# Attention with a low-rank FFN on one core: where the row maxima are turned, and which of three PSUM banks each product gets

## What is computed

```
def attention(q, k, v):                      # q: layernorm(x), k = v = context
    qh = q.reshape(B, S, KV, G, D)           # KV 8, G 4, D 32, S 512
    scores = einsum('bkgsd,bktd->bkgst', qh, kh) / sqrt(D)
    return einsum('bkgst,bktd->bkgsd', softmax(scores), vh)
x = x + attention(layernorm(x), ctx, ctx)
x = x + ffn(layernorm(x))   # gates of 8 experts, the best one's rank-8 update, bias, debias
```

## Time and profile before

| | us |
|---|---|
| median of 3 runs (lowest to highest) | 1023.52 (1023.04 to 1024.38) |
| the profiled execution's own time | 1017.48 |
| its span, first to last instruction | 1015.7 |
| busy: PE 940.9, DVE 901.5, POOL 801.3, ACT 726.1 | of 1015.7 |

### The profile page before, as it was taken

One profiled execution on the slowest core, in us unless ns is written; L12 is line 12 of the kernel. 1 busy time (PEld: TensorE's weight loads), 2 busy tenths in 40 slices (PEclk: granted clock), 3 DMA queues, 4 the chain that ended last, 5 costly groups with the idle time before them and its releaser, 6 DMA issues.

```text
span 1015.7 us, 24586 instructions
## 1 busy us (share of the span) xinstructions
PE 940.9 (93%) x9518; PEld 368.9 (36%) x9518; DVE 901.5 (89%) x1106; ACT 726.1 (71%) x1301; POOL 801.3 (79%) x454
## 2 busy tenths in 40 slices
PE   4799999999999999999999999999999999999996
PEld 3223333333333333333333323333222225777773
DVE  6979999999999999999999999998888886888877
ACT  5378888888888888887777777788777777554440
POOL 7269999999999999999999999998999998322210
PEclk9789999999999999999999999999999999999999
DMA  7685686768676768676767686756556744766424
GB/s 248 198 179 122 149 184 143 178 137 184 139 176 148 182 133 187 134 177 147 185 142 174 141 185 132 182 121 153 120 123 138 163 92 152 236 222 221 169 109 165
DMA packets 319875, 164.18 MB, mean 162 GB/s; under 512 B 182216, under 2 KB 307240, under 8 KB 319760
## 3 DMA queue, kind: packets, MB, share of 16 engines
q1 hardware_dynamic: 319456, 161.76, 64.8%
q0 software_dynamic: 304, 0.85, 0.4%
HBM read 107.58 MB, written 54.53 MB: 160 GB/s over the span
## 4 chain that ended last, share of the span: by engine, by line
PE 36%; DVE 30%; issue 24%; ACT 5%; POOL 3%; DMA 0%; SPq 0%; DVEq 0%; POOLq 0%; ACTq 0%
DVE row_max L927 14%; PE psum L590 8%; PE psum L604 6%; PE psum L617 5%; PE psum L735 4%; DVE den_t L939 4%; PE psum L552 4%; ACT probs L864 4%; PE psum L713 3%; DVE o_t L933 2%; DVE probs L1138 2%; PE psum L578 2%; DVE prod_mem L985 2%; PE psum L701 1%; ACT prod_mem L817 1%
## 5 line engine op out<-in xcount | busy, mean ns | idle before, releaser
L864 ACT ACTIVATE probs<-psum 128x512 f32<-128x512 f32 x1024 | 552.8, 596 | 134.9 <-PE psum L590 121.7
L927 DVE TENSOR_REDUCE row_max<-psum 128x4 f32<-128x2048 f32 x248 | 565.1, 2279 | 65.9 <-PE psum L552 65.5
L590 PE MATMUL psum<-q_stack,k_stack 97*32 97x512 f16 x4096 | 329.7, 386 | 7.7 <-ACT probs L864 2.1
L353 POOL TENSOR_TENSOR sums<-probs 128x2048 f32<-128x2048 f32 x63 | 287.3, 4561 | 17.4 <-ACT probs L864 17.4
L365 POOL TENSOR_TENSOR sums<-probs 128x2048 f32<-128x2048 f32 x63 | 287.9, 4570 | 13.0 <-ACT probs L864 12.9
L604 PE MATMUL psum<-probs,v_in 128*32 128x512 f32 x2048 | 268.2, 598 | 3.9 <-ACT probs L864 0.2
L590 PEld LDWEIGHTS psum<-q_stack,k_stack 97*32 97x32 f16 x4096 | 91.4, 94 | 219.6 <-ACT probs L864 131.4
L552 PE MATMUL psum<-high_mem 32*128 32x512 f16 x992 | 98.2, 385 | 23.6 <-DVE row_max L927 20.0
L325 POOL TENSOR_TENSOR o_t<-o_t,inv 128x512 f32<-128x512 f32 x64 | 67.2, 1050 | 32.1 <-DVE inv L945 32.1
L604 PEld LDWEIGHTS psum<-probs,v_in 128*32 128x32 f32 x2048 | 58.1, 110 | 87.2 <-issue 54.3
L330 POOL TENSOR_TENSOR o_all<-o_all,o_t 128x512 f32<-128x512 f32 x64 | 81.5, 1273 | 9.2
(11 more groups left out here) (119 smaller groups left out, 762.4 us busy)
## 6 DMA issues: line engine op xcount, KB each, us to landing
q_stack<-q_split SPq DMA_DIRECT2D x192, 128.0 KB, 3.5
xa<-in_x_dram SPq DMA_DIRECT2D x32, 512.0 KB, 4.9
o_all<-in_x_dram SPq DMA_DIRECT2D x256, 64.0 KB, 2.4
x_attended<-o_all SPq DMA_DIRECT2D x64, 256.0 KB, 4.2
out_dram<-probs SPq DMA_DIRECT2D x32, 512.0 KB, 2.8
q_split<-prod_mem SPq DMA_DIRECT2D x15, 1024.0 KB, 5.3
xa<-x_attended SPq DMA_DIRECT2D x16, 512.0 KB, 4.4
probs<-x_attended SPq DMA_DIRECT2D x16, 512.0 KB, 4.7
```

The source lines that it names most:

```text
L353: pool.tensor_tensor(sums[:, (2 * u - 1) % SUMS], probs[:, (u - 1) % 2, 2], probs[:, (u - 1) % 2, 3], ALU.add).then_inc(back_done, 1)
L590: last = pe.matmul(st_ps[row:row + D, bank_of["score", u, n], :], k_stack[:, u % SLOTS, t * P + row:t * P + row + D], q_stack[:, u % SLOTS ...
L864: act.activation(probs[:, s, keys, g, :], st_ps[:, bank_of["score", u, n], :], ACT.Exp, scale=EXP_SCALE).then_inc(exped, 1)
L927: dve.reduce_max(row_max[:, u % 2, t:G * ST:ST], s_ps[:], AX.X).then_inc(reduced, 1)
```

## The change

`turn_max(u+1)` moves, in TensorE's third quarter, from behind the gather to right behind the maxima product; `make_shift` moves in ScalarE's stream from the middle of the third quarter's exponentials to the beginning of that quarter, ahead of the part's high half. The planner is rewritten: instead of counting uses (a score keeps its bank for 2 further uses, a part for 6), it gives each use a time in quarters and a number of quarters that it is kept (0.4 for a score or the maxima, 0.95 for a part; denominators until a given point of the next unit), and a tile's second and third part need no longer be in the bank of the part before. Nothing is computed otherwise.

```
-            filled = [("part", n, i) for n in range(FIRST) for i in range(PIECES)]
+            QUARTERS_KEPT = {"score": 0.4, "max": 0.4, "part": 0.95}
+            DEN_TAKEN_AT = (ST + 0.95, 3.95)
+            filled = [(-LEAD, ("part", n, i)) for n in range(FIRST) for i in range(PIECES)]
...
-                    if u % 2 == 1 and t < PIECES and whole(tile_of(u)):
-                        filled.append(("part", tile_of(u), t))
-                    filled += scores[:half]
-                    if t == 2 and live(u + 1):
-                        filled.append(("max", u + 1, 0))
-                    filled += scores[half:]
+                    now = []
+                    if t == 2 and live(u + 1):
+                        now.append(("max", u + 1, 0))
+                    if u % 2 == 1 and t < PIECES and whole(tile_of(u)):
+                        now.append(("part", tile_of(u), t))
+                    now += scores
...
+                    filled += [(u * ST + t + (i + 1) / (len(now) + 1), use) for i, use in enumerate(now)]
...
-                if use[0] == "part" and use[1] >= FIRST and use[2] > 0:
-                    bank = bank_of["part", use[1], use[2] - 1]
...
-                kept = KEPT["den"][use[1] % 2] if use[0] == "den" else KEPT[use[0]]
-                free_at[bank], last_in[bank] = max(i, free_at[bank]) + kept + 1, use
+                if use[0] == "den":
+                    free_at[bank] = (use[1] + 1) * ST + DEN_TAKEN_AT[use[1] % 2]
+                else:
+                    free_at[bank] = max(at, free_at[bank]) + QUARTERS_KEPT[use[0]]
+                last_in[bank] = use
...
@@ tensor
+                        if t == 2 and 0 < u + 1 < UNITS:
+                            turn_max(u + 1)
                         if u % 2 == 1 and t < PIECES and whole(tile_of(u)):
                             turn_part(tile_of(u), t)
...
                             gather(u, t - 1)
-                        if t == 2 and 0 < u + 1 < UNITS:
-                            turn_max(u + 1)
@@ scalar
+                        if t == 2 and live(u + 1):
+                            make_shift(u + 1)
                         if u % 2 == 1 and t < PIECES and whole(tile):
                             high_part(tile, t)
...
-                                if n == MIDST[u % 2][2] and live(u + 1):
-                                    make_shift(u + 1)
```

More of the change, by code:

```diff
@@ L204, in xattn_ffn @@
                     scores = [("score", u, n) for n in range(BEGIN[u % 2][t], BEGIN[u % 2][t + 1])] if live(u) else []
-                    half = MIDST[u % 2][t] - BEGIN[u % 2][t]
+                    now = []
+                    if t == 2 and live(u + 1):
+                        now.append(("max", u + 1, 0))
                     if u % 2 == 1 and t < PIECES and whole(tile_of(u)):
-                        filled.append(("part", tile_of(u), t))
-                    filled += scores[:half]
-                    if t == 2 and live(u + 1):
-                        filled.append(("max", u + 1, 0))
-                    filled += scores[half:]
+                        now.append(("part", tile_of(u), t))
+                    now += scores
                     if t == (ST - 1 if u % 2 == 1 else 2) and live(u - 1):
-                        filled.append(("den", u - 1, 0))
-            KEPT = {"score": 2, "max": 2, "den": (5, 5), "part": 6}
-            bank_of, bank_before, free_at, last_in = {}, {}, [0] * BANKS, [None] * BANKS
-            for i, use in enumerate(filled):
+                        now.append(("den", u - 1, 0))
+                    filled += [(u * ST + t + (i + 1) / (len(now) + 1), use) for i, use in enumerate(now)]
+            bank_of, bank_before, free_at, last_in = {}, {}, [-LEAD] * BANKS, [None] * BANKS
+            for i, (at, use) in enumerate(filled):
                 bank = min(range(BANKS), key=lambda b: free_at[b])
-                if use[0] == "part" and use[1] >= FIRST and use[2] > 0:
-                    bank = bank_of["part", use[1], use[2] - 1]
                 bank_of[use] = bank
@@ L865, in _ @@
                                                scale=EXP_SCALE).then_inc(exped, 1)
-                        elif t == 2 and live(u + 1):
-                            make_shift(u + 1)
                 def copy_yT(q, t):
```

## The result

The changed kernel takes 1008.84 us (median of 4 runs, 1008.09 to 1009.29), the kernel before beside it 1023.28 us (4 runs, 1017.98 to 1024.38): 0.9866 of it, with a 95% interval of 0.9848 to 0.9884. The profiled execution took 1008.09 us. Against the profiled execution of before (1017.48) that is 9.4 us, which looks like the forecast.

What follows compares the result with a forecast made beforehand. VectorE (23.59 us) and TensorE (24.23) were both near their limit in a 25.30 us pair. Pairs 7.5, late pairs 0.1 and unit 0 1.0 sum to 8.6, taken as 8.7: 1023.52 to 1014.8 us, range about 1011 to 1020.5.

Steps and rivals of the forecast that it cites:

- odd unit, 25 times: Odd unit's third and fourth quarter: maxima product and gather come sooner, gaining 0.28 us (0.17 to 0.38) per unit.
- even unit, 25 times: Even unit's third quarter: 0.21 + 0.06 - 0.29 = -0.02 us, bounds -0.23 to +0.05.
- late pairs: The six pairs without a part, behind the 25: only the even unit's term counts, 0.1 us.
- three banks in unit 0: Unit 0: a third bank removes scores' standing for exponentials, 0.5 us at each of two places, 1.0 us (0 to 1.2).
- none is waited for in the pair, so I cost them at nothing: SyncE's queue: shift's DMA up to 1.4 us (even) and 2.0 us (odd) sooner, what queues behind it too; counted as nothing.
- I charge 0.20 us: Odd unit: cost of the turned maxima running ahead of the part, bounds 0.10 and 0.31 us.
- neighbouring consideration: Odd unit: changing tiling mode drains TensorE, so turned maxima would cost 0.12 us, not 0.20; total about 2 us better.
- for a reason that the profile cannot show: Base: timed median 1023.52 us lies 6.04 us above the profiled execution, unexplained; the gain was taken from the median.
- its lower end, about 1011: Fast end of the range: 1023.5 - 25 x 0.45 - 1.2, about 1011 us.
- The slower rival: Odd unit's score 9 waits for a late shift, holding TensorE, from 0.78 us of lateness; about 1027 us, chance 0.06.
- the brake on ScalarE: Odd unit: exponentials 8 and 9 slip by 0.31 us or more, only 3 to 4 us gained, 1019.5 us; chance 0.18.
- A stretch at half clock: From the nothing-moves rival (0.10): a second such stretch in the run costs up to 8.5 us, eating the gain; 1023 us.

Runs made afterwards that it cites:

- even_only: The kernel before with the turned maxima moved in even units alone, banks by the old rules: 1018.57 us, 0.9961.
- plan_only: The kernel before with only the new planner, turned maxima and shift's copy in their old places: 1023.24 us, 1.0009.
- shift0_sooner: The kernel before with only ScalarE's copy of unit 0's shift put ahead of the part's high half: 1018.76 us, 0.9968.
- move_old_start: The kernel before with both moves and the old planner, but unit 0's shift copy left behind the part's high half: 1007.94 us, 0.9856.
- move_only: The kernel before with only the moves of the turned maxima and the shift's copy, old planner's bank rules: 1005.36 us, 0.9827.
- three_banks: The kernel before with both moves, old planner, unit 3's load behind unit 1's shift, and unit 0's scores in three banks: 1002.92 us, 0.9807.
- unit3_later: The changed kernel with unit 3's first load taken out of SyncE's start and put behind unit 1's shift: 1007.6 us, 0.9854.
- before_profiled: The kernel before, unchanged, run once more for a second profile: 1021.41 us, 0.9989, profiled at 1022.17 us.
- max_bank: The changed kernel with an odd unit's turned maxima taking the second bank to come free instead of the first: 1006.69 us, 0.9841.

## Why the prediction was wrong

The mechanism was right: the odd unit's waits are the ones named, the shift hides, ScalarE is no brake, and nothing in the pair waits for the shift. The sum was too small. By its terms:

| term | forecast, us | shown, us | by |
|---|---|---|---|
| odd unit, 25 times | 25 x 0.28 = 7.0 | 25 x 0.31 = 7.8 | timeline after |
| even unit, 25 times | 25 x 0.02 = 0.5 | 25 x 0.10 = 2.5 | even_only, timeline after |
| late pairs | 0.1 | 0.5 | six times 24.09 to 24.00 |
| three banks in unit 0 | 1.0 | 0 | plan_only |
| SyncE, unit 0's shift | 0 | 3.3 (1.6 to 4.8) | shift0_sooner, move_old_start |
| sum | 8.6, taken as 8.7 | 14.1 | measured 14.4 by the medians, 13.7 (11.9 to 15.6) by the ratio |

The pairs' terms are firm to a tenth; the 3.3 us are not, so the sum's closeness to the measured time is partly luck.

- **The step that failed most** is "none is waited for in the pair, so I cost them at nothing". It is true in the pairs and was carried to the start, where SyncE's queue has no pause and each issue behind unit 0's shift, unit 1's shift among them, inherits its time. A DMA is hidden only as long as its queue has slack, and I looked for slack where the kernel spends its time, not where it begins. By the medians the effect is larger than the 0.3 to 0.9 us by which unit 1's shift goes out sooner (58.13, against 58.45 and 59.05 in the two profiles of before); how long TensorE stands and whether a stretch at half clock follows go with it. How the 3.3 us divide between the start and the tail is not settled: against the second profile of before, that of shift0_sooner is 2.2 us shorter up to unit 2 and 1.2 in the tail, against the recorded one 0.5 shorter and 1.7 longer. Without this term the others give 10.8 us, about 1012.5, inside the range.
- **The even unit** gave 0.10 us and not 0.02. Every row that I read was right (0.33, 0.21, 0.06 measured as 0.07); the term left out is the 0.08 us of the first denominators, which stood for the bank of the turned maxima. I followed what is queued behind the moved instruction, and not who takes its bank next. The explanation by the bank rests on the rows and the bank tables; the experiment shows only that the gain belongs to the even half.
- **The odd unit**: "I charge 0.20 us" for the turned maxima ahead of the part was too much, they cost 0.12. Exactly that stood in the neighbouring consideration by the Trainium skill, page "TensorEngine Tiling (Array Packing)", section Key Properties; the trace agrees with the number, 440.05 to 440.17, and no run isolates the reason. The maxima product came 0.18 us sooner for 0.11 forecast, the following one 0.31 for 0.28, and VectorE's idle time fell to 0.39 and 0.22 for 0.46 and 0.18.
- What the prediction took as given, that the turned maxima must wait for the low half, is the changed planner's choice and costs the 0.12 us. With the old rules (move_only) the odd half gives 0.44.
- **Unit 0**: "so both count: 1.0 us" failed. VectorE did wait for TensorE there, but behind it stood a third party, the shift of unit 1 in SyncE's queue, which took the gain (the stand of 4.86 us in plan_only). Where that was out of the way, three_banks shows 0.5 us that is the banks' and up to 1.25 together with a sooner rise of the clock; whether 1.0 was the right size is open.
- **The base**: that the profiled execution lies 6 us under the median "for a reason that the profile cannot show" was given up too early. Its windows show 4.7 us of it beside a second profile: no stand of 2.8 us at the start and no half clock in the tail. The forecast of the span, about 1007 with 1006.3 measured, was right by luck: the gain was forecast too small, and the execution that it was taken from was faster than most.
- **The range**: its lower end, about 1011, was worked out with 0.45 us a pair, though the bound given for a pair was 0.61; with 0.61 and the same 1.2 it is about 1007, and the measured time lies inside. The slower rival's 1027 does not follow from its terms either: at 1 us of lateness, with 0.40 of slack and the 0.30 gained, they give about 1031. Nothing rests on that one.
- **The rivals**: for the brake on ScalarE to hold, exponentials would have had to slip; six run in a row from 441.33. For the slower case the shift would have had to come 0.78 us late; its copy starts 0.30 us behind the turned maxima's start (440.05) and is done at 440.62, ahead of the high half. A stretch at half clock does exist at 60.8, but the kernel before has one as well in its second profile.

## What to carry to other kernels

Cost a change to a queue at nothing only where the queue is seen to pause, and look at the start apart from the steady state: there one DMA that goes out sooner moves everything behind it, and a load taken out of the way of one transfer may land in front of the next, as in unit3_later. When an operation moves, follow its buffer as well as its engine: who had to wait for it, and which use it must now wait for; a planner that picks banks by time of release alone can put a cheap instruction behind a late reader although a free bank stands beside it. And take a second profile of the baseline, or at least split it into stretches, before a difference of two profiles is read as a gain.

## What the runs showed of the hardware

- The tail, the same instructions in all these kernels, comes in three lengths: 186.12 us in the recorded profile of before with no stretch at half clock, 187.53 in that of the changed kernel with one of 3.4 us, 189.10 in before_profiled with one of 6.8 us. The other eleven profiles fall beside one of the three (185.9, 187.2 to 187.8, 188.7 to 189.1). What decides which one comes is open; it would account for 3 of the 6 us over which the runs of one kernel spread.
- Seven stands of TensorE for unit 1's shift, 2.28 to 4.86 us long, were each followed by 3.4 or 6.8 us at half clock, three of 0.69 to 1.25 us by none; but the stand of 2.39 us for unit 2's shift in unit3_later was followed by none.
- A shift's transfer of 4 KB landed 2.3 to 2.8 us behind its issue for unit 1, but for unit 2 anywhere from 1.7 us (before_profiled, plan_only, max_bank) to 4.6 (move_only), with 3.7 in the changed kernel and in unit3_later. Why it varies is open.
- In the windows before the first record of the clock PEclk reads 1.00, though the durations tell of half clock. The first maxima products of the changed kernel take longer than the later ones of the same shape, the first of these lines against the second:

```profile
47.56 0.61 PE L544 MATMUL psum<-high_mem 32*128 32x512 f16 x4
...
51.37 0.40 PE L554 MATMUL psum<-high_mem 32*128 32x512 f16 x4
```
